# Sixteen dummy products behind the slots, a reordered start of both expert stages, and an earlier mask in a four-stage attention and expert kernel

## What is computed

```python
x = x + attention0(norm(x), ctx)    # softmax over the context rows, a pooled row, then (4*256 -> 256)
x = x + experts0(norm(x))           # 8 experts 256 -> 512 -> 256 (silu) and 4 that return their input, top 2 of 12
x = x + attention1(norm(x), ctx, mask)   # 4 heads of 64, masked softmax
x = x + experts1(norm(x))           # 8 experts 256 -> 1024 -> 256 (gelu), own scale and shift, top 2 of 8
```

## Time and profile before

| | us |
|---|---|
| median of 3 runs | 1006.76 |
| lowest and highest | 1002.62, 1009.89 |
| the profiled execution | 1015.48 |
| its span, first to last instruction | 1013.5 |
| granted clock of TensorE, mean | 0.946 |

### The profile page before, as it was taken

One profiled execution on the slowest core, in us unless ns is written; L12 is line 12 of the kernel. 1 busy time (PEld: TensorE's weight loads), 2 busy tenths in 40 slices (PEclk: granted clock), 3 DMA queues, 4 the chain that ended last, 5 costly groups with the idle time before them and its releaser, 6 DMA issues. The chain is left out here.

```text
span 1013.5 us, 19644 instructions
## 1 busy us (share of the span) xinstructions
PE 897.1 (89%) x6186; PEld 793.2 (78%) x6187; DVE 624.3 (62%) x1395; ACT 516.6 (51%) x1107; POOL 434.9 (43%) x374
## 2 busy tenths in 40 slices
PE   5899999858999995679899999987579999999996
PEld 4798988737899984468787787875269999999995
DVE  6876452484566664588778778775845444455443
ACT  5645231343344452577586686665625555555552
POOL 1374251004566661746164263220125555555642
PEclk9999999867999997789999999999879999999998
DMA  9621000455666736701020000007936666777662
GB/s 296 230 84 42 1 2 1 155 173 189 217 236 226 256 117 194 156 21 42 1 64 21 22 22 1 27 1 237 346 115 189 193 199 200 207 206 198 197 183 51
DMA packets 69651, 134.74 MB, mean 133 GB/s; under 512 B 8112, under 2 KB 51760, under 8 KB 64464
## 3 DMA queue, kind: packets, MB, share of 16 engines
q1 hardware_dynamic: 56240, 110.27, 32.4%
q0 software_dynamic: 13344, 23.63, 10.6%
HBM read 109.08 MB, written 21.64 MB: 129 GB/s over the span
## 5 line engine op out<-in xcount | busy, mean ns | idle before, releaser
L1807 ACT ACTIVATE x<-d_hps,b 128x128 f32<-128x128 f32 x312 | 88.9, 368 | 126.4 <-PE d_hps L1903 126.4
L1903 PEld LDWEIGHTS d_hps<-d_xg_t,d_xw 128*128 128x128 f32 x1248 | 148.1, 195 | 4.0 <-DVE d_xg_t L2084 2.6
L1903 PE MATMUL d_hps<-d_xg_t,d_xw 128*128 128x128 f32 x1248 | 148.6, 278 | 1.9 <-DVE d_xg_t L2084 1.9
L879 POOL TENSOR_SCALAR c_prob<-c_prob,c_rinv 128x1024 f32<-128x1024 f32 x64 | 72.0, 1141 | 130.4 <-DVE c_rinv L1338 130.0
L1913 PE MATMUL d_yps<-d_w,d_hid_hi 128*128 x312 | 116.7, 406 | 3.3 <-DVE d_hid_lo L2093 3.3
L1732 POOL DMA_INDIRECT out_x<-d_y,d_take_slot x39 | 63.1, 1619 | 108.8 <-DVE d_y L2121 99.8
L2084 DVE TENSOR_SCALAR d_xg_t<-d_take,ln_w,ln_b 128x128 f32<-128x128 f32 x78 | 28.4, 406 | 99.7 <-PE d_take L1892 92.4
L1345 DVE TENSOR_TENSOR c_pt_lo<-c_tp,c_pt_hi 128x512 fp32r<-128x512 f32 x128 | 82.3, 683 | 6.1 <-ACT c_pt_hi L1167 5.8
L1903 PEld LDWEIGHTS b_hps<-b_xg_t,b_w 128*128 128x128 f32 x624 | 80.1, 202 | 6.4 <-issue 3.6
L1903 PE MATMUL b_hps<-b_xg_t,b_w 128*128 128x128 f32 x624 | 81.1, 286 | 3.7 <-issue 3.0
L1331 DVE CUSTOM_DVE_ANT_0 c_prob<-c_sc,c_minf 128x1024 f32<-128x1024 f32 x64 | 75.6, 1219 | 11.0 <-PE c_sc L964 10.9
(11 more groups left out here) (376 smaller groups left out, 2184.2 us busy)
## 6 DMA issues: line engine op xcount, KB each, us to landing
d_xw<-in_w SPq DMA_DIRECT2D x39, 1024.0 KB
b_w<-in_w SPq DMA_DIRECT2D x47, 512.0 KB, 7.7
d_w<-in_w SPq DMA_DIRECT2D x8, 1024.0 KB, 12.0
a_raw<-in_ctx_t SPq DMA_DIRECT2D x8, 512.0 KB, 7.2
a_raw<-in_ctx SPq DMA_DIRECT2D x8, 512.0 KB, 4.3
ybuf<-a_zero SPq DMA_DIRECT2D x2, 2048.0 KB
k_stage<-in_ctx_t SPq DMA_DIRECT2D x12, 256.0 KB, 3.1
rows<-b_xn_all SPq DMA_DIRECT2D x1, 2048.0 KB, 12.8
```

What stands on the lines that cost most here:

```text
L879: nc.gpsimd.tensor_scalar(prob[w][:], prob[w][:], rinv[:, w:w + 1], 1.0, ALU.mult, ALU.mult).then_inc(s["prob_ready"], 1)
L1807: op = nc.scalar.activation(hid[q][:, h * FH + c, :], src[:, c, :], ACT.Gelu_apprx_tanh, bias=b1[:, ds(e, 1), h * FH + c])
L1903: mm = nc.tensor.matmul(hps[j % 2][h][:, c * P:(c + 1) * P], w1[j % WL][:, k, at:at + P], xg_t[j % 2][:, k, :], start=(k == 0), stop=(k == ...
```

## The change

Four edits. Attention 1 has 22 dummy products in place of 12 ahead of its wait for the normalised rows. The load of the first mask goes from block 31 to block 29, and the four mask tiles go from behind scatters 34 to 37 to behind scatters 32 to 35. Both expert stages have sixteen in place of eight dummy products behind the slot products. In both expert stages DVE makes all low parts of the last experts' weights between `take_in(0)` and `take_in(1)`.

```diff
--- before.py
+++ after.py
@@ -1009,7 +1009,7 @@
             pe.wait_ge(s["k_lo"], 2)
             v_proj(2, av[:])
             v_proj(3, xb[:])
-            for _ in range(12):
+            for _ in range(22):
                 nc.tensor.matmul(tp[0][:], ctx_hi[:, 0, 0:P], ctx_hi[:, 0, 0:S], start=True, stop=True)
             pe.wait_ge(s["xn_ready"], TB)
             for k in range(KD):
@@ -1686,7 +1686,7 @@
             for n in range(WL, NB):
                 sp.wait_ge(s["up_done"], 4 + 2 * (n - WL) + 2)
                 load_w1(n)
-                if first and n == NB - TB - 4:
+                if first and n == NB - TB - 6:
                     m.first_mask(sp)
                 if first and n == WL + 1:
                     sp.dma_start(raw[:, 0:4, :].rearrange("p (k h) j -> p k (h j)", k=KD),
@@ -1745,8 +1745,8 @@
                 if n + GATHERS < NB:
                     gather(n + GATHERS)
                 scatter(n)
-                if first and NB - TB - 1 <= n < NB - 1:
-                    m.first_mask_tile(pool, n - (NB - TB - 1))
+                if first and NB - TB - 3 <= n < NB - 3:
+                    m.first_mask_tile(pool, n - (NB - TB - 3))
                 if not first and n + LANES < NB:
                     take_gate(n + LANES)
 
@@ -1883,7 +1883,7 @@
                 mm = nc.tensor.matmul(slots[:, 0:2 * NBX], in_lane[:, n, :], val[:, n, :, :].rearrange("p a b -> p (a b)"),
                                       start=(n == 0), stop=(n == 2 * T - 1))
             mm.then_inc(s["slots_done"], 1)
-            warm(8, rank)
+            warm(16, rank)
 
             def turn_in(n, j, turn):
                 pe.wait_ge(gathered[j % GATHERS], turn(j, GATHERS) * 16 + 16)
@@ -2120,13 +2120,10 @@
                     dve.wait_ge(gate_in[j % LANES], turn(j, LANES) * 16 + 16)
                     V.tensor_scalar(y[j % LANES][:], yb[:], gate_slot[:, ds(n, 1)], None, ALU.mult).then_inc(s["y_ready"], 1)
 
-            ahead = len(DVE_LAST) - 3
-            for e in DVE_LAST[:max(ahead, 0)]:
+            take_in(0, 0)
+            for e in DVE_LAST:
                 weights_low(e)
-            take_in(0, 0)
             take_in(1, 1)
-            for e in DVE_LAST[max(ahead, 0):]:
-                weights_low(e)
             hidden_low(0, 0)
 
             row_of = lambda rows, t: rows[:, ds(t, 1), :].rearrange("p a d -> p (a d)")
```

## The result

| | before | after |
|---|---|---|
| median, us | 1007.65 (9 runs, 1002.62 to 1014.56) | 1001.60 (9 runs, 997.26 to 1005.24) |
| ratio of the two | | 0.9931, 95% interval 0.9905 to 0.9957 |
| the profiled execution, us | 1015.48 | 1000.10 |
| its span, us | 1013.5 | 998.0 |

The change gains 6.05 us between the medians, and the interval of the ratio leaves anything from 4.3 to 9.6 us; the forecast said 6.2. The two profiled executions lie further apart, 15.5 us of span, because that of before was a long one (7.8 us over its median) and that of after a short one (1.5 us under). So the pair of traces shows where things moved, but not how much of it is there in every execution, and much of what follows is about telling the two apart.

The account below looks back on a forecast made before the run. PE, busy for 89% of the span, was taken as the bound, with time to gain only at three stage borders. The terms, -4.2 - 0.9 - 1.9 + 0.8 = -6.2 us, took the 1006.76 us median to 1000.6; range 993 to 1007.5.

Parts of the forecast that it names:

- part 1: End of experts 0: mask tiles behind scatters 32 to 35 let the last scatter go earlier; -4.2 us.
- part 2: Start of attention 1: 22 dummies keep the clock up, so the transposes run at 2.4 GHz; -0.9 us.
- part 4: Start of experts 1: new order delays the second products, which may lose the clock, and removes a later wait; +0.8 us.
- Part 3: Start of experts 0: sixteen dummies may bring the clock up before the first products; -1.9 us, between -4.3 and +1.1.
- (a): Clock rises at experts 0 and the new order pays at experts 1: -10.9 us, to 995.9 us; chance 0.2.
- (b): Start of attention 1 is held by something else, such as accumulating transfers: +0.6 us, or 1007.4 us; chance 0.22.
- (c): End of experts 0: POOL's mask turns stretch beside DVE; kernel 10 us slower with losses at the experts, 1016.8 us; chance 0.03.

Follow-up runs that it names:

- e1: The kernel before with only the mask's load and tiles two blocks earlier (also called e1_mask): 1003.25 beside 1008.71 us for before, ratio 0.9949.
- e3: The kernel before with only sixteen instead of eight dummies in both expert stages: 1008.00 beside 1008.71 us for before, ratio 0.9992.
- e4: The kernel before with only the new order of the weights' low parts in both expert stages: 1007.97 beside 1008.71 us for before, ratio 1.0001.
- e2: The kernel before with the earlier mask and 22 instead of 12 dummies in attention 1: 1004.69 beside 1008.71 us for before, ratio 0.9965.
- e9: The kernel after with two low parts ahead of the first take, 38 dummies in experts 1 and attention 1's raw load in three parts: 994.70 us, ratio to before 0.9862.
- e10: e9 with 12 instead of 22 dummies in attention 1: 993.34 us, ratio to before 0.9850.
- e12: The kernel after with 12 instead of 22 dummies in attention 1: 1002.00 beside 1009.34 us for before, ratio 0.9927.
- e11: The kernel after with eight instead of sixteen dummies in both expert stages: 1003.47 beside 1007.07 us for before, ratio 0.9956.
- e5: The kernel after with the old order of the low parts in experts 1 only: 1001.62 beside 1007.31 us for before, ratio 0.9935.
- e6: The kernel after with attention 1's raw load in three parts, behind the weights of blocks 4, 5 and 6: 997.72 beside 1007.31 us for before, ratio 0.9888.
- e8: The kernel after with two low parts ahead of the first take and 38 dummies in experts 1: 995.28 beside 1007.31 us for before, ratio 0.9867.

## Why the prediction was right, and where it was not

The sum was right, 6.2 against 6.05 us, and the mechanism behind its largest term too: the mask on POOL held the last scatter, and with it the start of attention 1. Term by term it was less exact. That the sum agrees to 0.2 us is luck: part 1 was about 1 us too small, part 2 promised 0.9 us that no pair shows, part 4 had the wrong sign, and the interval of the result is 5 us wide.

**Part 1, -4.2 expected, -5 to -5.5 measured (e1).** The scatter moved nearly as worked out, 3.6 to 3.8 us against 4.2: in the kernel after the two bare scatters stand 1.70 and 1.28 us behind the ones before them and not 1.31, and the four turns take 16.11 us and not 15.92. What was mis-sized is the way from the scatter to SP's fetch, taken over as 4.28 us: it is 2.50 to 2.66 in all eleven profiles with the early mask, and with the old one it was 4.28, 4.09 and 2.77. So the late mask doesn't always go with a long way (e3, 2.77), and the 1.7 us are not shown to be due to the edit. In before and in e4 the transfer engines moved nothing in the first 1.5 us behind the issue (0 GB/s; 11 GB/s in e3). Why wasn't tried.

**Part 2, -0.9 expected, 0 to +1.4 measured (e1 and e2, e9 and e10, e12).** The step that failed is "only 1.7 us are idle, so I expect the transposes at 2.4 GHz", as a gain of the 22. The clock over the transposes came back by part 1 alone, because twelve dummies leave just 1.32 us (e1) and 1.41 (e12), not 4.0; only in e10, with 2.40 us, did it fall in part. The 0.9 us at POOL exist (from the transposes to POOL's rows 6.61 us before, 5.50 in e1), but belong to part 1. "The transposes, at 394.4, are not held" came true only just in the profile of after, where the dummies end 0.04 us ahead of the rows; in e2 and four other profiles with 22 they are held by 0.2 to 0.7 us.

**Part 3, -1.9 expected, -1.9 to -2.5 in company (e11), -0.7 alone (e3).** The mechanism is right: the clock rose inside the dummies, at 229.0, and it was up for the first products in all nine profiles with sixteen (2.05 us each), and down for most of them in all five with eight (3.40 to 3.79 us). The size agrees by the medians, though the intervals of e11 and after overlap. The row's measure, 9.99 to 5.97, is 4 us, and the median shows about half. "They cost nothing", said of the low parts between the takes, missed that their place can also let the early clock through (7.42 us in e3's profile against 5.97). The Trainium skill, "TensorE: Matmul & The Clock Gate" (part 1, on the clock gate), speaks of a rise that varies from run to run. The profiles with eight dummies agree: 9.99, 8.37, 9.75, 7.31 and 10.00 us for the same stretch, while with sixteen and the new order all lie between 5.77 and 5.97.

**Part 4, +0.8 expected, -1 to -2 at the place, nothing sure in the whole (e4, e5).** Here the sign was wrong. The second products did start late (11.1 us behind the first transposes, 9.4 before) and did lose the clock, and the old wait of 3.34 us was gone, all as forecast. What was mis-sized is the price of the lost clock: "up to 3.5 us more" against 5.47 - 3.84 = 1.6, since the clock was back within these products (1.00 from 737.7). So the down products started 0.3 us sooner than before and not up to 2.1 later, and won back 4.45 - 2.88 = 1.6 us, close to the forecast's upper limit of 1.7: 21.27 - 19.42 = 1.9 us in all.

**What was missed altogether** is the wait for the weights of block 5 and the clock behind it (e6). It can't be seen in the page's 40 slices, each 25 us long, and no part of the change touches it, but it moved by up to 3 us from execution to execution, and most of the odd 2.5 us between the two profiles' blocks lies there.

**The rivals.** (a), everything paying at once, describes the one profile of after well (first products at 2.4 GHz, stretch at experts 1 shorter), but not the median. (b) is out: SP's fetch, the sums and POOL's chain all followed (first line 879 at 49.83 us behind scatter 32, 56.00 before). (c) is out: the mask's turns in the kernel after took 4.07, 3.68, 3.69 and 4.67 us, all under 5.0. The longest mask operation there was 1.54 us, in the last turn, so a tile can be slow for a reason that wasn't tried; of the rule in the Trainium skill, "GPSIMD Engine Reference" (specifications), on the interface shared with VectorE, no run here isolates anything.

## What to carry to other kernels

When work is moved off the path, look at what the moved item stood in front of, and then ask again of every filler that was sized for the old wait: ten more dummies showed no gain once most of the wait had gone, and held the engine in five of eight profiles. Fill a strict queue's idle time before it takes from the busy side: two subtractions ahead of the first take gave more (about 4 us) than the reorder under study. And before a small change is judged by one pair of profiles, look at the same stretch in several: here a single pair showed 15.5 us where the medians show 6.

## What the runs showed of the hardware

The time of one and the same kernel moved by several us between executions: the kernel before lay between 1002.62 and 1014.56 us in nine runs, the kernel after between 997.26 and 1005.24. The profiles, one of each kernel, show places where it can arise: the clock over the first products of experts 0 (3.40 to 3.79 us for the same 16 products behind eight dummies, 2.05 behind sixteen), the wait for the weights of block 5 with the clock behind it (0 to 2.95 us), and the way from the last scatter's issue to SP's fetch, 2.5 to 4.3 us for the same 128 KB. They are not the only ones: from the transposes of line 925 to the first transposes of experts 1 it took 334.0 to 337.9 us in the fourteen profiles, which wasn't looked into.

Whether a kernel that keeps the clock at such a place is steadier too is not shown. e8 lay between 993.53 and 996.51 us in five runs, but e1_mask, with eight dummies, also lay within 4.4 us in eleven.
